# A hybrid transformer block on one core: the 88 products of local attention in 22 sets of four instead of 24 of four and three, with new planner offsets

## The chip, the cores and the metric

The kernel is one program on one core of a Trainium2 chip. The metric is device time in microseconds (us) of one execution. TensorE (PE in the rows; PEld is its weight load), VectorE (DVE), ScalarE (ACT), GpSimd (POOL) and SyncE (SP, which only issues DMAs here) each run their own instruction list and meet at semaphores.

## What is computed

Eight batches of 512 x 256 pass a local attention (stage A), an expert feed-forward (F), a causal attention (B) and the feed-forward again, each with a layer norm before it. The change lies in A:

```python
_OFFSETS = list(range(41)) + [128, 96, 384]      # 44 offsets
idx = arange(T)[:, None] - deltas[None, :]       # T = 512
k_mod = k[:, :, max(idx, 0)] * (1.0 + scale_embed)
scores = einsum('bhtd,bhtjd->bhtj', q, k_mod) / sqrt(HD) + pos_bias    # H = 16, HD = 16
scores = where(idx >= 0, scores, finfo.min)
out = einsum('bhtj,bhtjd->bhtd', softmax(scores), v[:, :, max(idx, 0)]) * if_gain
```

## The kernel before

Stage A is called once per batch (eight calls), B eight times, F sixteen times. In A, channels stand on partitions, in two halves (hf) of 8 heads. For each of the 44 offsets (slots) and each half, VectorE multiplies qT by kT shifted by the offset, 512 columns: 88 products per call (L1302 to L1308). Four of them (or three) are one set: one VectorE instruction makes all near slots of a set (their offsets are equally spaced, so one access pattern reads them), and each far slot (41 to 43) needs its own. TensorE then sums each product over the 16 channels of a head with the narrow weights slot_w, 32 columns wide, into one quarter of a bank's partitions (L1623 to L1627): the products of a set use different column tiles of the array and run together. Each matmul is two instructions (fp32). A bank holds a group of up to 16 slots: 4 column tiles by 4 rounds, 8 heads each, so 128 partitions. The third group has 12 slots, laid out as 3 column tiles by 4 rounds, on 96 partitions (GROUP_J, L22; PRODUCTS, L66; SETS, L70). The last set of a group is followed by a matmul of is_slot and ahead, which puts -1e30 where t is less than the offset (L1632); ScalarE then copies the bank to sT with the position bias (L1086). There are 24 sets in a call, 16 of four and 8 of three.

Then for each of four tiles of 128 rows, "tS": TensorE turns the three groups of each half (L1600), VectorE takes the maximum per head over 44 slots (L1262) and subtracts it (L1265), ScalarE takes the exponential ("p"), SyncE writes the near slots to a band in DRAM (L897) and reads it back skewed (L909), GpSimd adds the far slots, and TensorE multiplies the turned weights with V.

Product buffers: sets 0 to 5 alternate between two, later sets between four (SET_AT, L75), and a product waits until TensorE has used the set that was there (L1301).

The order of every engine's instructions is made ahead by a planner in the file (ordered(), L498): each phase has an estimated time per engine (local_phases(), L149), and a list scheduler picks the next block by its earliest start, rounded to TICK, and then by its rank times DEPTH plus fixed pulls per phase (PULL) and per call (CALL_PULL). Calls of A, B and F interleave by this: while one batch's attention makes products, another's experts use TensorE. The planner also gives each result one of eight PSUM banks. The setup makes slot_w from a mask and the scales (L1483).

Of the kernel before, what the change touches and what calls it, by code (L numbers as in the profile page):

```python
# [21 lines left out]
GROUP_J = [16, 16, 12]  # L22
NG = len(GROUP_J)
# [21 lines left out]
def columns(names):  # L45
    at, n = {}, 0
    for name, w in names:
# [18 lines left out]
PRODUCTS = [(hf, g, col, r) for hf in range(2) for g in range(NG) for r in range(4) for col in range(GROUP_J[g] // 4)]  # L66
# [4 lines left out]
        for hf in range(2) for g in range(NG) for r in range(4)]  # L71
# [8 lines left out]
def slot(n):  # L80
    _, g, col, r = PRODUCTS[n]
    return 16 * g + 4 * col + r
# [66 lines left out]
def local_phases():  # L149
# [14 lines left out]
    for q, of in enumerate(SETS):  # L164
# [4 lines left out]
        p.put(("prod", q), ("DVE", 0.067 * len(runs(q)) + 0.534 * len(of), *needs), ("PE", 0.9 if r < 3 else 1.3 if g == NG - 1 else 1.1))  # L169
        if r == 3:  # L170
            p.put(("sT", hf * NG + g), ("ACT", 0.58, ("prod", q, "PE")))
# [4 lines left out]
    for kind, i in TILES:  # L176
        if kind == "tS":
            p.put(("tS", i), ("PE", 0.62, ("v", 1, "PE"), *[("sT", g, "ACT") for g in range(2 * NG)]),
                  ("DVE", 2.0, *([("write", i - 2, "DMA"), ("far", i - 2, "POOL"), ("far_den", i - 2, "DVE")]
                                 if i >= 2 else [])))  # L180
        elif kind == "p":
            p.put(("p", i), ("ACT", 0.68, ("tS", i, "DVE")))
            p.put(("write", i), ("SP", 0.4, ("p", i, "ACT")), ("DMA", 2.6))
            if i > 0:
                for k in (0, 1) if i == 1 else (i,):
                    p.put(("read", k), ("SP", 0.4, ("write", k, "DMA"),
                                        *([("pA", k - 2, 3, "PE")] if k >= 2 else []),
                                        *([("pB", k - 2, 1, "PE")] if k >= 3 else [])), ("DMA", 7.0))
# [142 lines left out]
def calls():  # L331
# [19 lines left out]
TICK, DEPTH = 0.02, 1.55  # L351

PULL = {
    ("A", "DVE"): {"prod": 3430, "on": 470, "pB": 170},
    ("A", "PE"): {"tS": 780, "on": 990, "oNT": 350},
    ("B", "ACT"): {"mT": -1390, "ST": -2340},
    ("B", "DVE"): {"qk": 280, "S": -80, "on": -680},
    ("B", "PE"): {"turn": 1070, "qk": 2960, "S": 4290, "mT": 130, "ST": 1930, "oNT": 1020, "pr": 170},
    ("F", "ACT"): {"gexp": -20},
    ("F", "DVE"): {"stats": 1490, "xn": -150, "cont": -1470, "lg": -300, "gates": -810},  # L360
    ("F", "PE"): {"turn": -620, "hid": 316, "eo": 1710, "dec": 10230},
}
CALL_PULL = {
    "A": [-7420, 0, 0, -510, -460, -300, -60, -157],
    "B": [300, 810, 340, 0, 300, 450, 640, -260],
    "F": [0, 910, -390, 0, -80, 0, -30, 0, 130, 670, 370, 0, 296, 650, 0, 0],
# [249 lines left out]
SLOTS_SETUP, TABLES_SETUP = 5, 11  # L616
DVE_SETUP = 26
# [26 lines left out]
def build(nc, x_dram, kept_dram, setup_dram, out_dram):  # L644
# [9 lines left out]
    with ctx:  # L654
# [179 lines left out]
        def products_used(u, q):  # L834

            if q % 4 == 3:
                return bank_full(u, ("sT", q // 4))
            return nth(u, "prod_used", q - q // 4 + 1)
# [213 lines left out]
        def _(act):  # L1052
# [15 lines left out]
            def local_attention(u, name):  # L1068
# [13 lines left out]
                elif kind == "sT":  # L1082
                    rows = GROUP_J[i % NG] * HPT
                    act.wait_ge(*bank_full(u, name))
                    ps, read = place(u, name)
                    nc.scalar.activation(sT[0:rows, i, :], ps[0:rows, :], ACT.Identity,  # L1086
                                         bias=c("pos_bias", i, 1)[0:rows, :]).then_inc(read, 1)
# [111 lines left out]
        def _(dve):  # L1199
# [51 lines left out]
            def softmax_local(u, i):  # L1251
# [4 lines left out]
                for hf in range(2):  # L1256
                    dve.wait_ge(*bank_full(u, ("tS", i, hf)))
                    ps, read = place(u, ("tS", i, hf))
                    s = ps[:, 0:J * HPT].rearrange("p (j h) -> p j h", j=J)
                    halves.append((s, read))  # L1260
                    m = mx[:, i, hf * HPT:(hf + 1) * HPT]
                    link(u, nc.vector.tensor_reduce(m, s.rearrange("p j h -> p h j"), AX, ALU.max))  # L1262
                for hf, (s, read) in enumerate(halves):
                    m = mx[:, i, hf * HPT:(hf + 1) * HPT]
                    nc.vector.tensor_tensor(p_nat[:, i % 2, :, hf * HPT:(hf + 1) * HPT], s,  # L1265
                                            m.unsqueeze(1).broadcast_to([P, J, HPT]), ALU.subtract
                                            ).then_inc(read, 1)
# [642 lines left out]
```

## Time and profile before

| | us |
|---|---|
| median of 3 runs | 1737.67 |
| lowest, highest | 1734.58, 1738.28 |
| the profiled execution | 1734.03 |
| its span | 1731.9 |
| TensorE busy | 1580.9 (91%) |
| VectorE busy | 1282.0 (74%) |
| ScalarE busy | 787.8 (45%) |
| mean granted TensorE clock | 0.977 of full |

One execution is profiled. A row of the grouped lines names the source line, engine, output and inputs, shape and count, then the busy time together, the mean of one instruction, and the engine's idle time before them with what ended it. Instructions of one engine overlap by their start and end, so the distance between starts is shorter than the duration.

### The profile page before, as it was taken

Reading aid. Unit: us, or ns where it says so; the run is one execution under the profiler, and the core shown is the slowest. Engines: PE = TensorE matmul, PEld = TensorE weight load, DVE = VectorE, ACT = ScalarE, POOL = GpSimd, SP = SyncE. Lnnn points to the kernel's source line nnn. Section 1 sums busy time; section 2 is a strip of 40 time slices with the busy share of each in tenths; the row PEclk is TensorE's granted clock in tenths of the full one; section 3 lists DMA queues with packets and bytes.
Section 4 is the critical chain, followed back from the end, with each engine's and each line's share of the span. In section 5 each row is a group of like instructions: output and inputs, shape, how many; then the busy total and the mean of one; then the engine's idle time right before and its main releaser. Section 6 shows DMA issues by size and latency. Waiting matters only on the chain. (4 is left out here: it accounts for less than half of the span.)

```text
span 1731.9 us, 28223 instructions
## 1 busy us (share of the span) xinstructions
PE 1580.9 (91%) x10560; PEld 882.0 (51%) x10560; DVE 1282.0 (74%) x3138; ACT 787.8 (45%) x1474; POOL 141.6 (8%) x155
## 2 busy tenths in 40 slices
PE   6599899999999999999999999999989998997976
PEld 2164465546555465554654556454655546454533
DVE  7969757896569966798767976699666996746633
ACT  1134346445364544644355353644536444552633
POOL 1010110101101020000101011010200001000000
PEclk9899999999999999999999999999999999998989
DMA  9230440014301161022500244001520216013000
GB/s 318 79 121 1 159 148 2 16 73 172 86 3 39 50 219 40 2 87 86 172 2 15 75 141 117 2 16 74 184 75 3 74 50 207 5 39 111 3 13 13
DMA packets 50261, 133.96 MB, mean 77 GB/s; under 512 B 6256, under 2 KB 22576, under 8 KB 45520
## 3 DMA queue, kind: packets, MB, share of 16 engines
q1 hardware_dynamic: 50128, 132.16, 23.3%
q8 instruction: 87, 1.43, 0.3%
q14 instruction: 46, 0.38, 0.1%
HBM read 80.99 MB, written 46.04 MB: 73 GB/s over the span
## 5 line engine op out<-in xcount | busy, mean ns | idle before, releaser
L1306 DVE TENSOR_TENSOR arena_AB<-qT,kT 128x2048 f32<-128x2048 f32 (+3 forms) x240 | 400.1, 1719 | 11.9 <-PE bank L1625 5.5
L1361 DVE CUSTOM_DVE_ANT_0 bank<-bank,causal_b 128x512 f32<-128x512 f32 (+3 forms) x512 | 234.1, 525 | 105.4 <-PE bank L1697 104.9
L1543 PE MATMUL bank<-arena_F,kept 128*128 128x512 f32 x512 | 235.6, 609 | 7.2 <-DVE arena_F L1451 4.8
L1625 PE MATMUL bank<-arena_AB,slot_w 128*32 128x512 f32 x1408 | 198.1, 612 | 32.6 <-DVE arena_AB L1306 31.4
L1135 ACT ACTIVATE arena_AB<-bank 128x512 f32<-128x512 f32 (+1 forms) x352 | 167.0, 585 | 70.2 <-PE bank L1713 69.8
L1168 ACT ACTIVATE arena_F<-bank,kept 128x512 f32<-128x512 f32 x256 | 159.0, 688 | 20.0 <-PE bank L1543 17.7
L1543 PEld LDWEIGHTS bank<-arena_F,kept 128*128 128x128 f32 x512 | 96.5, 195 | 124.7 <-issue 113.1
L1543 PE MATMUL bank<-cont_hi,by_cont 128*128 128x512 f32 (+1 forms) x272 | 115.9, 426 | 9.6 <-DVE arena_AB L1361 6.5
L1821 PE MATMUL bank<-kept,arena_F 128*128 128x256 f32 x512 | 117.0, 382 | 7.1 <-ACT arena_F L1185 6.6
L1543 PE MATMUL bank<-xnT,kept 128*128 128x512 f32 x256 | 120.0, 622 | 2.2 <-ACT xnT L1060 1.5
L1806 PE MATMUL bank<-arena_F,kept 128*64 128x512 f32 x512 | 120.5, 602 | 0.4 <-ACT arena_F L1181 0.2
L1001 POOL TENSOR_TENSOR rstd_F<-var_eps_F,minus_half 128x4 f32<-128x4 f32 x32 | 40.2, 1256 | 973.8 <-DVE var_eps_F L1236 973.8
L1821 PEld LDWEIGHTS bank<-kept,arena_F 128*128 128x128 f32 x512 | 95.2, 190 | 26.5 <-ACT arena_F L1185 10.4
L1459 DVE TENSOR_TENSOR arena_F<-bank,kept 128x512 f32<-128x512 f32 x32 | 22.1, 691 | 116.8 <-PE bank L1821 116.8
L1543 PE MATMUL bank<-cont_lo,by_cont 128*128 128x512 f32 (+1 forms) x272 | 107.1, 394 | 0.0
L1709 PE MATMUL bank<-arena_AB 99*128 99x256 bf16 (+3 forms) x512 | 103.8, 301 | 0.2
L1625 PEld LDWEIGHTS bank<-arena_AB,slot_w 128*32 128x32 f32 x1408 | 35.2, 109 | 133.6 <-DVE arena_AB L1306 69.6
L1732 PE MATMUL bank<-arena_AB,V_b 128*32 128x512 f32 (+3 forms) x1024 | 87.1, 441 | 10.4 <-ACT arena_AB L1135 8.8
L1697 PE MATMUL bank<-arena_AB 96*128 96x512 bf16 (+3 forms) x512 | 89.3, 310 | 7.4 <-DMA arena_AB<-ones_b 4.1
L1713 PE MATMUL bank<-causal_T,ident_b 128*128 128x128 bf16 (+2 forms) x352 | 86.0, 244 | 0.0
L1543 PEld LDWEIGHTS bank<-xnT,kept 128*128 128x128 f32 x256 | 50.7, 202 | 60.6 <-issue 56.5
L1152 ACT ACTIVATE arena_F<-bank,half_enc_b 128x512 f32<-128x512 f32 x64 | 44.0, 687 | 79.9 <-PE bank L1543 79.9
(186 smaller groups left out, 2359.9 us busy)
## 6 DMA issues: line engine op xcount, KB each, us to landing
arena_AB<-band SPq DMA_DIRECT2D x32, 1344.0 KB, 6.6
arena_AB<-stacks SPq DMA_DIRECT2D x64, 384.0 KB
stacks<-arena_AB SPq DMA_DIRECT2D x48, 256.0 KB, 2.6
band<-arena_AB SPq DMA_DIRECT2D x32, 328.0 KB, 3.9
stacks<-xnT SPq DMA_DIRECT2D x32, 256.0 KB, 2.6
band<-kT SPq DMA_DIRECT2D x4, 1352.0 KB, 23.1
stacks<-xn SPq DMA_DIRECT2D x16, 256.0 KB, 3.0
kept<-kept_pack SPq DMA_DIRECT2D x1, 3765.0 KB, 18.8
```

The costliest lines, as they stand in the source:

```text
L1135: nc.scalar.activation(p_T[:, n % RS, cols[0]:cols[-1] + 1, 0:w], ps[:, 0:len(cols) * w].rearrange("p (c q) -> p c q", c=len(cols)), ACT.E ...
L1168: nc.scalar.activation(hid[:, n % RH, :], ps[:], ACT.Relu, bias=c("be1", n, 1)).then_inc(read, 1)
L1306: ins = nc.vector.tensor_tensor(prod[SET_AT[i]][:, col:col + c, :], qT[:, hf, :].unsqueeze(1).broadcast_to([P, c, T]), k, ALU.mult)
L1361: ins = nc.vector.tensor_tensor_reduce(out=s, in0=s, in1=causal[:, (TT - 1 - i) * P:T], scale=-1.0, scalar=BIG, op0=ALU.add, op1=ALU.min, ...
L1543: ins = nc.tensor.matmul(out(ps), w, x, start=n == 0, stop=n == len(pairs) - 1)
L1625: ins = nc.tensor.matmul(ps[HS * col:HS * (col + 1), :], slot_w[:, slot(n), :], prod[SET_AT[i]][:, col, :], start=r == 0, stop=False, skip ...
L1697: ins = nc.tensor.matmul(ps[:, at:at + (i + 1) * P], stacks[0:K, h // 4, 0, h % 4, i * P:(i + 1) * P], stacks[0:K, h // 4, 1, h % 4, 0:(i ...
L1709: nc.tensor.matmul(ps[:, at * w:(at + 1) * w], stacks[0:K + 3, g, 1, col, k * P:(k + 1) * P], stacks[0:K + 3, g, 0, col, k * P:T], start=a ...
L1713: ins = nc.tensor.matmul(ps[:, 0:number * w].rearrange("p (c q) -> p c q", c=number)[:, :, 0:P], ident_b[:], causal_T[:].unsqueeze(1).broa ...
L1732: ins = nc.tensor.matmul(ps_o[HS * col:HS * (col + 1), k * P:T], V_b[:, k, columns_of(4 * g + col)], p_T[:, n % RS, col, 0:w], start=k == ...
L1806: ins = nc.tensor.matmul(ps[M * e:M * (e + 1), :], we2[:, 2 * n + e, k, :], hid[:, (4 * n + 2 * e + k) % RH, :], start=k == 0, stop=k == 1)
L1821: ins = nc.tensor.matmul(ps[:, i * D:(i + 1) * D], t_moe[:, k, at:at + P], dec_w[:, k, :], start=k == 0, stop=k == KF - 1)
```

## The change

The third group gets four column tiles of three rounds (ROUNDS = [4, 4, 3]). All sets have four products; there are 22 in a call. Slot number, key stride (3 instead of 4 in that group), the last set of a group (LAST) and the semaphore counts follow. The third group's scores now stand on all 128 partitions, 24 of each 32 in use; the unused 8 get a bias of -1e30, so that they are never the maximum. Score transposes, mask matmul and ScalarE's copy lose their 96-row special case. VectorE's maximum reads 384 columns, and its subtraction becomes two instructions, 32 slots and 12 slots, so that p_nat keeps its 44 slots. The planner gets times for band writes and reads per tile, and other TICK, DEPTH, PULL and CALL_PULL.

```diff
 GROUP_J = [16, 16, 12]
+ROUNDS = [4, 4, 3]
...
-PRODUCTS = [(hf, g, col, r) for hf in range(2) for g in range(NG) for r in range(4) for col in range(GROUP_J[g] // 4)]
+PRODUCTS = [(hf, g, col, r) for hf in range(2) for g in range(NG) for r in range(ROUNDS[g]) for col in range(4)]
...
-        for hf in range(2) for g in range(NG) for r in range(4)]
+        for hf in range(2) for g in range(NG) for r in range(ROUNDS[g])]
+LAST = [q for q, of in enumerate(SETS) if PRODUCTS[of[0]][3] == ROUNDS[PRODUCTS[of[0]][1]] - 1]
...
-            p.put(("tS", i), ("PE", 0.62, ("v", 1, "PE"), *[("sT", g, "ACT") for g in range(2 * NG)]),
-                  ("DVE", 2.0, *([("write", i - 2, "DMA"), ("far", i - 2, "POOL"), ("far_den", i - 2, "DVE")]
+            p.put(("tS", i), ("PE", 0.66, ("v", 1, "PE"), *[("sT", g, "ACT") for g in range(2 * NG)]),
+                  ("DVE", 2.2, *([("write", i - 2, "DMA"), ("far", i - 2, "POOL"), ("far_den", i - 2, "DVE")]
...
-            p.put(("write", i), ("SP", 0.4, ("p", i, "ACT")), ("DMA", 2.6))
+            p.put(("write", i), ("SP", 0.4, ("p", i, "ACT")), ("DMA", (2.3, 2.3, 6.3, 5.0)[i]))
...
-                                        *([("pB", k - 2, 1, "PE")] if k >= 3 else [])), ("DMA", 7.0))
+                                        *([("pB", k - 2, 1, "PE")] if k >= 3 else [])), ("DMA", (6.6, 8.3, 6.0, 6.5)[k]))
...
-TICK, DEPTH = 0.02, 1.55
+TICK, DEPTH = 0.04, 2.0
...
-    ("A", "DVE"): {"prod": 3430, "on": 470, "pB": 170},
-    ("A", "PE"): {"tS": 780, "on": 990, "oNT": 350},
-    ("B", "ACT"): {"mT": -1390, "ST": -2340},
-    ("B", "DVE"): {"qk": 280, "S": -80, "on": -680},
-    ("B", "PE"): {"turn": 1070, "qk": 2960, "S": 4290, "mT": 130, "ST": 1930, "oNT": 1020, "pr": 170},
-    ("F", "ACT"): {"gexp": -20},
-    ("F", "DVE"): {"stats": 1490, "xn": -150, "cont": -1470, "lg": -300, "gates": -810},
-    ("F", "PE"): {"turn": -620, "hid": 316, "eo": 1710, "dec": 10230},
+    ("A", "ACT"): {"sT": 300},
+    ("A", "DVE"): {"prod": 2450, "pB": 20},
+    ("A", "PE"): {"tS": 593, "on": 850, "oNT": 720},
+    ("B", "DVE"): {"S": 810, "pr": -160},
+    ("B", "PE"): {"qk": 2210, "S": 2460, "ST": 1840},
+    ("F", "ACT"): {"hid": 10, "gb": 450},
+    ("F", "DVE"): {"stats": 1990, "lg": 80, "eo": -350},
+    ("F", "PE"): {"hid": 473, "dec": 11940},
 }
 CALL_PULL = {
-    "A": [-7420, 0, 0, -510, -460, -300, -60, -157],
-    "B": [300, 810, 340, 0, 300, 450, 640, -260],
-    "F": [0, 910, -390, 0, -80, 0, -30, 0, 130, 670, 370, 0, 296, 650, 0, 0],
+    "A": [-6730, 0, -154, -80, -72, 0, -3, 0],
+    "B": [0, 0, 0, 0, 0, 0, -1180, 0],
+    "F": [0, 0, -77, 0, 0, 0, 4, 0, 0, 0, 74, 0, 100, -360, 520, 0],
...
-                    nc.vector.tensor_tensor(p_nat[:, i % 2, :, hf * HPT:(hf + 1) * HPT], s,
-                                            m.unsqueeze(1).broadcast_to([P, J, HPT]), ALU.subtract
-                                            ).then_inc(read, 1)
+                    p = p_nat[:, i % 2, :, hf * HPT:(hf + 1) * HPT]
+                    nc.vector.tensor_tensor(p[:, 0:whole], ps[:, 0:whole * HPT].rearrange("p (j h) -> p j h", h=HPT),
+                                            m.unsqueeze(1).broadcast_to([P, whole, HPT]), ALU.subtract)
+                    nc.vector.tensor_tensor(
+                        p[:, whole:J].rearrange("p (c r) h -> p c r h", c=4),
+                        ps[:, whole * HPT:NG * P].rearrange("p (c r h) -> p c r h", c=4, r=4)[:, :, 0:ROUNDS[-1]],
+                        m.unsqueeze(1).unsqueeze(1).broadcast_to([P, 4, ROUNDS[-1], HPT]), ALU.subtract).then_inc(read, 1)
...
-                        k = bass.AP(k.tensor, k.offset, [k.ap[0], [4, c], [1, T]])
+                        k = bass.AP(k.tensor, k.offset, [k.ap[0], [ROUNDS[g], c], [1, T]])
...
-                        rows = GROUP_J[g] * HPT
-                        ins = nc.tensor.transpose(ps[:, g * P:g * P + rows], sT[0:rows, hf * NG + g, i * P:(i + 1) * P],
-                                                  ident[0:rows, 0:rows])
+                        ins = nc.tensor.transpose(ps[:, g * P:(g + 1) * P], sT[:, hf * NG + g, i * P:(i + 1) * P], ident)
...
-                        nc.tensor.matmul(ps[0:rows, 0:cut], is_slot[:, g * P:g * P + rows], ahead[:, 0:cut],
+                        nc.tensor.matmul(ps[:, 0:cut], is_slot[:, g * P:(g + 1) * P], ahead[:, 0:cut],
...
+    bias.reshape(4, HS, 2, NG)[:, HPT * ROUNDS[-1]:, :, NG - 1] = NEG
```

The maximum (L1262) changes its input to ps[:, 0:NG * P], and the slot weights of the setup (L1483) are made by two instructions, for 32 slots in rounds of four and for 12 in rounds of three.

## Rows read from the trace of the kernel before

**Rows 1.** the page, its busy times, share of the span, instructions.

```profile
PE 1580.9 (91%) x10560; PEld 882.0 (51%) x10560; DVE 1282.0 (74%) x3138; ACT 787.8 (45%) x1474; POOL 141.6 (8%) x155
```

**Rows 2.** stretches: us, then busy us and (instructions) of PE, PEld, DVE, ACT, POOL, PEclk, DMA.

```profile
43.30:86.60 43.30, 25.25 (x143) 8.49 (x141) 42.18 (x61) 6.28 (x9) 3.77 (x5) 0.85 0.25 79
...
346.40:389.70 43.30, 43.27 (x206) 19.60 (x206) 42.57 (x66) 17.37 (x29) 1.01 (x1) 1.00 0.19 73
389.70:433.00 43.30, 39.84 (x383) 27.86 (x380) 27.97 (x63) 22.72 (x42) 7.17 (x10) 1.00 0.49 172
...
952.60:995.90 43.30, 43.24 (x212) 22.64 (x209) 42.84 (x58) 17.10 (x30) 1.01 (x1) 1.00 0.20 75
...
1645.40:1688.70 43.30, 31.13 (x162) 15.90 (x160) 13.40 (x39) 14.45 (x29) 1.01 (x1) 0.88 0.04 13
...
86.60:1558.80 1472.20, 1394.44 (x9616) 787.29 (x9614) 1122.88 (x2747) 702.91 (x1317) 129.24 (x134) 0.99 0.23 75
```

**Rows 3.** all waits of PE, those of 90 to 1430 us, the product matmuls' busy row.

```profile
PE bank L1625 <- DVE arena_AB L1306: 31.4, 43, 2.7
PE bank L1551 <- DVE xn L1248: 12.5, 2, 9.6
PE bank L1551 <- DVE arena_F L1248: 12.3, 3, 5.6
...
PE bank L1625 <- DVE arena_AB L1306: 13.3, 21, 2.7
...
L1625 PE MATMUL bank<-arena_AB,slot_w 128*32 128x512 f32 x1408 | 198.1, 612 | 32.6 <-DVE arena_AB L1306 31.4
```

**Rows 4.** PE in order of time: start us, us, what, instructions, idle before.

```profile
384.90 1.06 PE L1625 MATMUL bank<-arena_AB,slot_w 128*32 128x512 f32 x6
385.89 0.65 PE L1806 MATMUL bank<-arena_F,kept 128*64 128x512 f32 x2
...
562.76 1.92 PE L1625 MATMUL bank<-arena_AB,slot_w 128*32 128x512 f32 x12
...
573.82 1.92 PE L1625 MATMUL bank<-arena_AB,slot_w 128*32 128x512 f32 x16
```

**Rows 5.** products on DVE: two forms of the grouped lines, one run in time.

```profile
L1306 DVE TENSOR_TENSOR arena_AB<-qT,kT 128x2048 f32<-128x2048 f32 x128 | 287.2, 2287 | 8.9 <-ACT kT L1076 3.4 <-PE bank L1625 3.2 <-PE bank L1713 1.8
...
L1306 DVE TENSOR_TENSOR arena_AB<-qT,kT 128x512 f32<-128x512 f32 x48 | 32.9, 686 | 0.0
...
362.02 15.50 DVE L1306 TENSOR_TENSOR arena_AB<-qT,kT 128x2048 f32<-128x2048 f32 x7
```

**Rows 6.** score transposes by shape, and weight loads of the mask matmul.

```profile
L1600 PE MATMUL bank<-kept,arena_AB 128*128 128x128 f32 x128 | 21.6, 280 | 3.2 <-DVE arena_AB L1265 2.6 <-ACT arena_AB L1086 0.7
...
L1600 PE MATMUL bank<-kept,arena_AB 96*128 96x96 f32 x64 | 16.1, 251 | 0.0
...
L1632 PEld LDWEIGHTS bank<-ahead,is_slot x48: 94/96/120, 31.1 to 1417.3; 128*128 128x128 bf16 x32, 128*96 128x96 bf16 x16
```

**Rows 7.** score subtraction, a 256-column subtraction's like, two subtractions in time.

```profile
L1265 DVE TENSOR_TENSOR arena_AB<-bank,arena_AB 128x352 f32<-128x352 f32 x64 | 30.6, 520 | 1.1
...
L1277 DVE TENSOR_TENSOR oN<-bank,arena_AB 128x256 f32<-128x256 f32 x32 | 13.6, 424 | 1.1
...
407.03 0.96 DVE L1265 TENSOR_TENSOR arena_AB<-bank,arena_AB 128x352 f32<-128x352 f32 x2
```

**Rows 8.** the first local call: VectorE in time, then one set on PE.

```profile
18.36 4.50 DVE L1306 TENSOR_TENSOR arena_AB<-qT,kT 128x2048 f32<-128x2048 f32 x2 [3.43 <-ACT kT L1076]
25.55 44.69 DVE L1306 TENSOR_TENSOR arena_AB<-qT,kT 128x2048 f32<-128x2048 f32 x28 [2.70 <-PE bank L1625]
...
38.91 1.07 PE L1625 MATMUL bank<-arena_AB,slot_w 128*32 128x512 f32 x8 [1.14 <-DVE arena_AB L1306]
```

**Rows 9.** us to landing of band writes (L897), then of band reads (L909).

```profile
DMA to landing us min/median/max: 2.2/3.9/8.4
...
DMA to landing us min/median/max: 5.5/6.6/9.2
```

## Prediction: what 22 sets of four do to the time

> **What bounds the kernel now.** I read the page's busy lines first [rows 1]: TensorE is busy 1580.9 of 1731.9 us, VectorE 1282.0. 151 us of TensorE idleness are left. Then the table by stretches [rows 2] says where: between 87 and 1559 us TensorE is busy 1394 of 1472 us, so 78 us of idleness lie there and 73 at the two ends. In the first product stretch (43 to 87 us) VectorE is busy 42.18 of 43.30 us and TensorE only 25.25: there VectorE bounds. In later product stretches (346 to 390, 953 to 996 us) both are full: TensorE 43.27 and 43.24, VectorE 42.57 and 42.84. In the score and band stretch behind (390 to 433 us) VectorE has 15 us of slack. Last, the waits of TensorE [rows 3]: product matmuls waited 31.4 us for VectorE's products in the whole run, but 13.3 us in 21 waits between 90 and 1430 us, where seven of the eight local calls have theirs. So outside the first call TensorE's work and VectorE's work both count, TensorE's a little more, and work moves between stretches only by the planner's order.
>
> **Part 1, two product sets fewer per call.** A set of three column tiles (6 matmul instructions) alone takes 1.06 us, one of four (8 instructions) 1.07 [rows 4, 8]. Two sets of three in a row take 1.92 us, two of four 1.92 [rows 4]. So a set costs 1.92 - 1.06 = 0.86 us in a row, and alone 0.99 (from its start at 384.90 to the next work's at 385.89), whatever its number of columns. Before, a call has 24 sets, 8 of them of three; after, 22 of four. TensorE loses 2 sets: 1.72 to 1.98 us per call; I take 1.85, as sets stand in both ways.
> The Trainium skill ("TensorEngine Tiling (Array Packing)", Key Properties) says that a change of tiling mode drains TensorE. By that each set that stood alone would give back a drain besides; the difference 0.99 - 0.86 = 0.13 us is all that the trace shows of one, and 1.85 lies inside it.
>
> **Part 2, VectorE's products.** The products stay 88. A full set in a row costs 2.20 us: seven end 15.50 us after the first starts, one takes 2.287, so (15.50 - 2.29) / 6 [rows 5]. 2048 elements against 512 differ by 2287 - 686 ns, or 1.04 ns per element, hence 2.13 us of elements and 0.07 fixed. In the third group a half had 7 instructions (3 columns; three times 2 and 1), and gets 6 (three times 3 and 1, since slots 41 to 43 are single). Saving 2 x 0.07 = 0.13 us per call.
>
> **Part 3, scores.** The third group's rows fill 128 partitions, the unused ones with a bias of -1e30, so score tiles get 384 columns. On TensorE a transpose of 96 rows takes 251 ns, one of 128 rows 280 [rows 6]: 8 per call by 0.029 = +0.23 us, and not under zero, since the weight load has 128 columns in both. The closing mask matmul gets 128 instead of 96 weight columns, its 384 moving columns stay; weight loads of both widths lie between 94 and 120 ns [rows 6]: nothing, at most 2 x 0.03. ScalarE's copy with bias gets 128 partitions for 96 and keeps its 512 columns: nothing.
> On VectorE the maximum reads 384 instead of 352 columns: 32 x 1.04 = 33 ns. The subtraction becomes two instructions of 256 and 96 columns; two of 352 in a row end 0.96 us after the first starts and one takes 0.52, so a step of 0.44 us holds 0.37 of elements and 0.07 fixed [rows 7]. The split adds 0.07 us. Upper bound: no overlap at all, a whole 256-column instruction 424 ns plus 96 columns scaled from there, 257 ns, against 520: +0.16. With 8 pairs per call: 8 x (0.033 + 0.07) = +0.82 us, at most 1.5. VectorE's net is 0.82 - 0.13 = +0.7 us per call, and almost all of it in the score stretch, not among the products.
> The Trainium skill ("VectorE: DVE Perf Modes", Side-by-side) speaks against the split: it gives each instruction some 150 cycles of start at 0.96 GHz, which would be an estimated 64 x 0.16 = 10 us for the 64 extra subtractions. The step above disagrees: all but 0.07 us lies under the instruction before [rows 7], so 64 x 0.07 = 4.5 us. By the page a quarter of the other 5.5 us, 1.4 us, would come on top of the sum below.
>
> **Part 4, setup and bookkeeping.** The slot weights come from two instructions instead of one, +0.1 us by the fixed part above. VectorE idles 3.43 us before the first product, waiting for the keys [rows 8]: hidden. Semaphore indices change, no new wait arises; product buffers are reused two and then four sets back as before.
>
> **Part 5, the planner.** The band writes get 2.3, 2.3, 6.3, 5.0 us instead of 2.6, the reads 6.6, 8.3, 6.0, 6.5 instead of 7.0; the trace has 2.2 to 8.4 (median 3.9) and 5.5 to 9.2 (median 6.6) [rows 9], so the planner's picture is nearer to the chip. But all pulls, the tick and the depth change too, so every engine's order changes, that of the other two stages as well; on SyncE and GpSimd each band write, read or far sum can come to stand behind another call's wait. No row prices a new order. From above: the waits of TensorE that a better order could take are 5 to 13 us per kind [rows 3]; I take -10 as the gain's end. From below: one badly placed normalisation costs up to 9.6 us (xn) or 5.6 us (the experts'), as the longest waits before the transposes show [rows 3]. I take 0, since no row speaks for either side.
>
> **Sum against the profiled execution** (span 1731.9, whole 1734.03 us). First call: VectorE bounds it, its products follow each other for 44.69 us while TensorE waits before each set [rows 8]; two sets less on TensorE give nothing, and of VectorE's +0.7 I take +0.5, as its score steps have TensorE's transposes to wait for, too. The seven others: TensorE -1.85 + 0.23 = -1.6 each, -11.3 together. 21 of their 168 sets waited for VectorE, and in the fullest stretches VectorE has under 1 us left, so I count 0.8 of it: -9.0. VectorE's +0.8 per call lies where it has slack, but on the chain score transposes, maximum, subtraction, exponent, band write, band read; I charge a quarter: +1.4. Sum -7.1, so 1726.9 for the profiled execution. It ran 3.6 us under the median of the three runs; against that median the sum gives 1737.67 - 7.1 = 1730.6. Rounded **1730.5 us**, -0.41%.
>
> **Rivals.**
> (a) *The sum holds, order neutral*: 1724 to 1734, around 1730.5. For it: the exactly equal times of the set of three and of four. Chance 0.48.
> (b) *The new order gains besides.* With the later band landings the planner no longer puts head transposes where TensorE waits for the band, and the other calls close up: -7 and another -8 to -10, 1720 to 1722. For it: the 78 us of idleness in the middle [rows 2]. Against it: no single wait kind there is over 13.3 us. Chance 0.16.
> (c) *VectorE is the true bound of the product stretches, TensorE's freed time becomes waits for products.* For it: the VectorE column in [rows 2]. Then the rows "matmul of products waited for VectorE" grow by some 10 us and the time stays: 1737.67 + 7 x 0.2 = about 1737 to 1739. Chance 0.16, within 0.2% of before.
> (d) *Slower: the new order breaks hand-overs at the normalisation.* The place: the VectorE queue, where the normalisation of the next call stands behind products or score maxima, and TensorE's first transposes wait for it. The price is 5.6 us each (the experts' longest [rows 3]) with the clock at its lower level behind: in the stretch from 1645 us, where TensorE has gaps, the mean granted clock is 0.88 of 2.4 GHz, part of it at 1.2, against 1.00 in the full ones [rows 2]. It decides from two such new gaps on: -7.1 + 11.2 = +4, 1742 us; with three 1747. For it: all offsets change at once and the calls' pulls are mostly zero now. Against: the sixteen expert calls of before show such gaps only at the ends. Chance 0.20.
> That the change does not do what it says (fewer TensorE sets) is next to impossible by the code; that it does so without shortening anything is (c).
>
> **How the numbers follow.** A difference of 0.2% (3.5 us) is about what a measurement of this kernel can tell from no change. (a) is nearly all faster, one part in twenty within 0.2%; (b) faster; (c) within; (d) slower but for a small part. Faster 0.63, same 0.18, slower 0.19. Range: from (b)'s lower half, 1719.5, to 1741.5, which takes in (c) and the near side of (d); left out are about 0.05 below and 0.12 above, with the case of three gaps.
>
> **What would show it right or wrong.** The product matmuls stay 1408 instructions, in 22 sets of 8 per call, and are busy for 198.1 - 14 = about 184 us. VectorE makes the products with 16 instructions fewer, all sets with 1536 or 2048 columns in the first. The product sets' times on VectorE fall by about 2 us in all. The subtraction shows 64 of 256 and 64 of 96 columns with a step of 0.07 us between. TensorE's busy time falls by 11 to 13 us to about 1569. If the span falls by less than that, TensorE's idle time has grown: in waits for products it is (c), in waits for normalised tiles (d). The granted clock of full stretches should stay 1.00. The prediction is wrong if the time moves while TensorE's busy time does not fall, or if the score transposes come over 20 us later behind the products.

## The result

The changed kernel takes 1743.0 us (median of 12 runs, 1741.2 to 1745.5) against 1737.7 for the kernel before, measured anew beside it: a ratio of 1.0034, 95% interval 1.0026 to 1.0042. Forecast were 1730.5 us and a range up to 1741.5. The kernel became slower, by 5.9 us by the ratio and 5.3 by the medians, where a gain of 7 was forecast.

The page of the changed kernel, its busy times (answers to [rows 1]):

```profile
span 1741.7 us, 28222 instructions
PE 1574.4 (90%) x10544; PEld 877.6 (50%) x10560; DVE 1288.8 (74%) x3187; ACT 791.2 (45%) x1474; POOL 143.9 (8%) x155
```

TensorE is busy 6.5 us less, the span is 9.8 us longer, so it idles 167 instead of 151 us. (The profiled execution of before lies 3.6 us under its median, that of the changed kernel 0.7 over it, so some 4 of the 9.8 us are the choice of executions.) The stretches of the changed kernel (columns as in [rows 2]):

```profile
43.30:86.60 43.30, 24.13 (x146) 7.63 (x143) 42.23 (x63) 6.19 (x9) 3.71 (x5) 0.84 0.17 54
...
346.40:389.70 43.30, 42.74 (x207) 20.52 (x206) 42.74 (x58) 19.15 (x34) 1.01 (x1) 1.00 0.20 73
389.70:433.00 43.30, 40.65 (x360) 26.93 (x357) 32.03 (x78) 22.53 (x41) 6.43 (x8) 1.00 0.46 168
...
952.60:995.90 43.30, 42.58 (x213) 21.51 (x212) 42.72 (x60) 16.16 (x29) 1.01 (x1) 1.00 0.22 82
...
86.60:1558.80 1472.20, 1382.12 (x9571) 780.97 (x9587) 1127.95 (x2785) 703.09 (x1312) 131.63 (x134) 0.99 0.23 75
```

Between 87 and 1559 us TensorE is busy 12.3 us less than before and idle 12.3 us more: nothing of what it was relieved of became progress there. In the two full product stretches VectorE is as full as it was (42.74 and 42.72 us for 42.57 and 42.84), TensorE a little less (42.74 and 42.58 for 43.27 and 43.24).

The groups of the changed kernel that answer to [rows 3, 6] (line, engine, what, count, then busy, mean ns, idle before):

```profile
L1636 PE MATMUL bank<-arena_AB,slot_w 128*32 128x512 f32 x1408 | 183.9, 613 | 37.4 <-DVE arena_AB L1316 36.0
...
L1612 PE MATMUL bank<-kept,arena_AB 128*128 128x128 f32 x192 | 24.1, 275 | 2.7 <-DVE arena_AB L1274 2.0 <-ACT arena_AB L1093 0.7
```

One half's subtraction in time (start us, us), which answers to [rows 7]:

```profile
402.55 0.42 DVE L1272 TENSOR_TENSOR arena_AB<-bank,arena_AB 128x256 f32<-128x256 f32 x1
402.89 0.25 DVE L1274 TENSOR_TENSOR arena_AB<-bank,arena_AB 128x96 f32<-128x96 f32 x1
```

The instructions cost what the forecast said: the sets 183.9 us for 184 expected, 14.2 less; the second part of the subtraction starts 0.34 us after the first, 0.27 of which are its 256 columns, so 0.07 is fixed. TensorE's busy time fell to 1574.4 us, though, and not to 1569. Two groups that the change does not touch grew, with unchanged counts and a longer mean. They are the matmuls of the experts' and of both attentions' normalised input; the changed kernel, then what they were before:

```profile
L1556 PE MATMUL bank<-arena_F,kept 128*128 128x512 f32 x512 | 239.8, 617 | 10.0 <-DVE arena_F L1461 5.0
...
L1556 PE MATMUL bank<-xnT,kept 128*128 128x512 f32 x256 | 124.0, 635 | 3.6 <-ACT xnT L1068 2.3
```

```profile
L1543 PE MATMUL bank<-arena_F,kept 128*128 128x512 f32 x512 | 235.6, 609 | 7.2 <-DVE arena_F L1451 4.8
...
L1543 PE MATMUL bank<-xnT,kept 128*128 128x512 f32 x256 | 120.0, 622 | 2.2 <-ACT xnT L1060 1.5
```

One execution each does not carry much here. In runs below that keep the order of before, the second group takes 120.0 to 123.8 us, and the new layout in the order of before has TensorE busy for 1573.0 us in one run and 1568.6 in another of the same time. The first group takes 235.6 to 236.8 us in the old order and 237.7 to 239.8 in four runs with the new numbers or their order, so 1 to 4 us of it may belong to them. Nor does the granted clock of single stretches tell the kernels apart: the changed kernel, the kernel before, and the kernel before with nothing but its subtraction split, whose order is that of before (a few us later in its work by then):

```profile
1472.20:1515.50 43.30, 41.18 (x179) 21.23 (x181) 30.71 (x115) 22.14 (x40) 0.00 (x0) 0.92 0.09 23
...
1472.20:1515.50 43.30, 42.26 (x198) 21.10 (x197) 31.08 (x117) 24.20 (x44) 0.00 (x0) 0.99 0.02 4
...
1472.20:1515.50 43.30, 41.39 (x190) 21.38 (x191) 33.11 (x131) 22.21 (x40) 1.02 (x1) 0.92 0.17 45
```

Over all runs the mean granted clock is 0.973 for the changed kernel (12 runs) and 0.976 for the kernel before (the 19 runs beside the first experiments). So a little more of TensorE's work met the lower level (1.2 GHz); how much of the 5 us that is stays open.

### The profile page after: what moved, and what is told of

Read it like the earlier page. It is cut to its first block and busy times, and to the rows that moved or that the text cites. A ratio compares the mean times of both kernels' runs of the same rounds, so it can differ in the third digit from the quotient of the medians.

```text
span 1741.7 us, 28222 instructions
## 1 busy us (share of the span) xinstructions
PE 1574.4 (90%) x10544; PEld 877.6 (50%) x10560; DVE 1288.8 (74%) x3187; ACT 791.2 (45%) x1474; POOL 143.9 (8%) x155
## 3 DMA queue, kind: packets, MB, share of 16 engines
q1 hardware_dynamic: 50128, 132.16, 23.1%
## 5 line engine op out<-in xcount | busy, mean ns | idle before, releaser
L1316 DVE TENSOR_TENSOR arena_AB<-qT,kT 128x2048 f32<-128x2048 f32 (+1 forms) x224 | 397.6, 1829 | 10.7 <-PE bank L1636 5.3
L1556 PE MATMUL bank<-arena_F,kept 128*128 128x512 f32 x512 | 239.8, 617 | 10.0 <-DVE arena_F L1461 5.0
L1636 PE MATMUL bank<-arena_AB,slot_w 128*32 128x512 f32 x1408 | 183.9, 613 | 37.4 <-DVE arena_AB L1316 36.0
L1556 PE MATMUL bank<-xnT,kept 128*128 128x512 f32 x256 | 124.0, 635 | 3.6 <-ACT xnT L1068 2.3
L1009 POOL TENSOR_TENSOR rstd_F<-var_eps_F,minus_half 128x4 f32<-128x4 f32 x32 | 44.1, 1379 | 1003.2 <-DVE var_eps_F L1242 1003.2
```

The lines of the kernel that those rows point to most:

```text
L1316: ins = nc.vector.tensor_tensor(prod[SET_AT[i]][:, col:col + c, :], qT[:, hf, :].unsqueeze(1).broadcast_to([P, c, T]), k, ALU.mult)
L1556: ins = nc.tensor.matmul(out(ps), w, x, start=n == 0, stop=n == len(pairs) - 1)
L1636: ins = nc.tensor.matmul(ps[HS * col:HS * (col + 1), :], slot_w[:, slot(n), :], prod[SET_AT[i]][:, col, :], start=r == 0, stop=False, skip ...
```

## The experiments

Two theories stood after the result. **Order**: the layout gains what the sum said and the new offsets cost more. **Layout**: the freed TensorE time can't be used and VectorE's added work decides.

### Layout and order apart

The first run takes the order of every engine and every bank from the planner of before, with its 24 sets, and drops one place of the third group; the second does the reverse. (Edits here and below are shortened; notes behind # are not in the files.)

```diff
+def moved(q):                                    # e5: places of the old plan to new sets
+    hf, k = divmod(q, 12)
+    ... {8: [8], 9: [], 10: [9], 11: [10]} ... else 11 + ...
+def moved(q):                                    # e6: places of the new plan to old sets
+    hf, k = divmod(q, 11)
+    return [12 * hf + x for x in {8: [8, 9], 9: [10], 10: [11]}.get(k, [k])]
```

> The new layout (22 sets of four, split subtraction, 384-column scores) in the instruction order of the kernel before: every engine's list and every bank is taken from the planner of before with its 24 sets, and the second of the four sets of the third group is left out of both lists, so that the other three keep their places. Theory 'order' (the layout gains what the sum said, the new offsets cost more): 1729 to 1732 us, ratio about 0.996, TensorE busy near 1569. Theory 'layout' (VectorE's 0.7 us per call and the larger products decide, the freed TensorE time is not usable): 1740 to 1744 us, ratio 1.002 to 1.004. In between, 1735 to 1739: the freed time is lost in waits, and only a part of the loss is the layout's.

> The other half: the old layout (24 sets, 16 of four and 8 of three) in the instruction order and with the banks of the changed kernel; the fourth set of the third group is put right behind the first of that group. Theory 'order': 1747 to 1752 us, since the layout's 7 us are missing as well. Theory 'layout': 1735 to 1739 us, as before.

Measured: the layout in the old order 1742.3 us (1.0029, 1.0016 to 1.0043); the old layout in the new order 1750.4 us (1.0082, 1.0065 to 1.0099). The first is what the layout theory expected, the second what the order theory expected, so neither holds alone. In the order of before the layout **costs 4.7 us** (5.0 by the ratio); in the order of the change it **gains 7.4** (1750.4 to 1743.0). Each layout does relatively better in the order that was planned for it, so these are prices in an order that fits one side only.

Then the planner plans each layout with the other's numbers:

```diff
-TICK, DEPTH = 0.04, 2.0         # e1: the changed kernel with all planner numbers of before
+TICK, DEPTH = 0.02, 1.55        # (PULL, CALL_PULL, write 2.6 and read 7.0 likewise)
...
-TICK, DEPTH = 0.02, 1.55        # e2: the kernel before with all planner numbers of the change
+TICK, DEPTH = 0.04, 2.0
```

> The new layout planned anew by the planner with the numbers of before: old tick, depth and pulls, old band landings. Theory 'order': the offsets were made for 24 sets, so the plan is another one, but 1730 to 1738 us, below the changed kernel. Theory 'layout': 1740 to 1745 us. A time above 1745 would say that the offsets only fit one plan, whatever the layout.

> The old layout planned anew with the tick, depth, pulls and band landings of the change. Theory 'order' (these numbers are worse in themselves): 1745 to 1752 us. Theory 'layout': 1736 to 1740 us. If it comes near 1743 as the changed kernel does, layout and numbers can't be told apart by replanning alone, and the pair that keeps an order decides.

Measured: 1733.9 us for the new layout with the old numbers (0.9984, 0.9974 to 0.9995) and 1763.1 us for the old layout with the new ones (1.0148, 1.0128 to 1.0168). With numbers that were not chosen for it, the new layout gains 3.8 us over the kernel before (2.8 by the ratio). **The changed kernel's own numbers cost it 9.1 us against the old ones** (1733.9 to 1743.0; the kernel before stood at 1737.6 and 1737.7 beside them). They are bad for the old layout too, by 25 us, more than either theory had expected (1745 to 1752 or less). Planning the new layout for itself, with the same old numbers, takes it from 1742.3 to 1733.9 us: the 4.7 us above are the price in an order that was made for the other layout. And the 3.8 us are those of one plan; plans of this layout range from 1727.5 to 1760.2 us below.

### What a microsecond is worth in the old order

Why does the layout cost 4.7 us in the old order? The page of that run, its waits for products (us, times, longest), and those of 90 to 1430 us:

```profile
PE 1573.0 (90%) x10544; PEld 879.8 (51%) x10560; DVE 1288.1 (74%) x3187; ACT 787.8 (45%) x1474; POOL 141.4 (8%) x155
```

```profile
PE bank L1678 <- DVE arena_AB L1358: 43.5, 59, 2.7
```

```profile
PE bank L1678 <- DVE arena_AB L1358: 26.1, 39, 2.7
```

TensorE waits 12 us more for products than in [rows 3], all of it in the middle, where the waits went from 13.3 us in 21 to 26.1 in 39. Four runs take the change apart. The first has the layout with VectorE's score work of before, the second the kernel before with the split subtraction, the others the kernel before with less work on one engine each:

```diff
-                    whole = 16 * (NG - 1)        # e7, on top of e5: one subtraction of 352
+                    nc.vector.tensor_tensor(p_nat[...], ps[:, 0:J * HPT]..., m..., ALU.subtract)
...
-                    nc.vector.tensor_tensor(p_nat[...], s, m..., ALU.subtract)      # e8
+                    for at, to in ((0, 32), (32, J)):
+                        ins = nc.vector.tensor_tensor(p_nat[:, i % 2, at:to, ...], s[:, at:to], m..., ALU.subtract)
...
-                    for n in SETS[i]:                                               # e10
-                        col = PRODUCTS[n][2]
+                    short = g == NG - 1 and r == 1
+                    for n in SETS[i][0:1] if short else SETS[i]:
+                        col, w_ = PRODUCTS[n][2], 64 if short else T
...
+                        w_ = T // 2 if g == NG - 1 and r == 1 else T                # e11
```

> The new layout in the order of before, but VectorE's score work as before: maximum over 352 columns and one subtraction of 352 (the 12 slots of the third group are then read from the wrong columns; the work is what counts). It takes 0.8 us per call off VectorE. Theory 'score chain' (the 4.7 us that the layout cost in this order are VectorE's added score work): 1735 to 1738 us. Theory 'products' (the cost is that the third group's products come in three larger portions and TensorE waits for them): 1740 to 1742 us, nearly as with the full layout.

> The kernel before with one edit: the subtraction in two instructions, 32 and 12 slots, 64 instructions more. Theory 'score chain': +3 to +5 us, 1741 to 1743. Theory 'products': 0 to +1 us. The step of the second subtraction behind the first should be 0.07 us beyond its elements; by the page that gives each instruction 150 cycles it would be 0.16 us.

> The kernel before with the summing of the second set of the third group left out but for one matmul of 64 columns: TensorE has 16 times some 0.7 us less, about 11 us, VectorE, order, waits and banks are untouched. If a microsecond of TensorE counts in the product stretch: 1729 to 1732 us. If VectorE's products set the pace there, as TensorE's 43.5 us of waits for products in the run with the layout alone suggest: 1735 to 1738 us, and the waits for products grow by 8 us or more.

> The counterpart: VectorE multiplies only 256 of 512 columns in the second set of the third group, 16 times 0.8 us, about 13 us less, and everything on TensorE is as before (the sums of the other half are then of an older product). If VectorE sets the pace of the product stretches: 1726 to 1731 us. If TensorE does: 1734 to 1738 us.

| run | VectorE busy | TensorE busy | ratio to before (95%) | us |
|---|---|---|---|---|
| layout, old score work | 1283.7 | 1575.7 | 1.0006 (0.9994 to 1.0017) | +1.0 |
| before, split subtraction | 1285.7 | 1581.0 | 1.0019 (1.0009 to 1.0029) | +3.3 |
| before, less on TensorE | 1281.6 | 1572.1 | 0.9974 (0.9962 to 0.9986) | -4.5 |
| before, less on VectorE | 1270.2 | 1579.6 | 0.9987 (0.9978 to 0.9997) | -2.3 |

Here and below us is the ratio's difference from 1 times 1737.5. The score chain is confirmed from both sides: taking VectorE's score work away returns 4.0 of the layout's loss, and the split alone, 3.7 us of VectorE, costs 3.3. That is some nine tenths (0.4 to 1.4 by the interval); the forecast charged a quarter. By which wait it costs that is not shown: TensorE's waits for products are 32.7 us with the split for 31.4 without, and those of the middle 26.0 us without the layout's score work for 26.1 with it. The run with less on TensorE falls between its two expectations: 8.8 us less busy gain 4.5, so half (0.3 to 0.75), where the forecast counted 0.8. Its waits (all, then 90 to 1430 us) show where the other half went:

```profile
PE bank L1626 <- DVE arena_AB L1306: 38.2, 52, 2.7
```

```profile
PE bank L1626 <- DVE arena_AB L1306: 20.0, 31, 2.7
```

6.8 us more waits for products than in [rows 3]. And 11.8 us less on VectorE gain only 2.3, a fifth (0.04 to 0.3), with TensorE's waits for products where they were, 31.6 us. So neither engine alone bounds the product stretch.

There remains a gap: with its score work taken away the layout should gain like the run with less on TensorE, 4.5 us or more, and stands at +1.0 (interval -1.0 to +3.0). The portions are different: the third group's four sets of three (VectorE 1.8 to 1.9 us each) became three of four (1753 + 685 ns, 2.4 us). Three runs look at that:

```diff
-    ... {8: [8], 9: [], 10: [9], 11: [10]} ...    # e15, on top of e5: another place left out
+    ... {8: [], 9: [8], 10: [9], 11: [10]} ...
...
+                    if (g, r) == (NG - 1, 1): ... 8 columns instead of the set's products and sums   # e16
...
+                        more = g == NG - 1 and r != 1 and run == runs(i)[-1]                          # e17
+                        c += int(more)
```

> As the run with the layout alone (1742.3 us), but of the third group's four places in the lists the first is left out, not the second: its three sets of four stand at the second, third and fourth. VectorE then has the time of four places for three larger portions. Theory 'portions' (TensorE comes to the larger portions before they are made): the waits for products fall from 43.5 towards 36 us, the time to 1738 to 1740. Theory 'place does not matter' (VectorE's sum of work counts): 1741 to 1744 us with the waits as they were.

> The kernel before with the second set of the third group left out on both engines (8 columns stay of it, so that waits and increments stand): VectorE 16 times some 1.6 us less, about 25 us, TensorE 16 times 0.8 us less, about 12. If the prices of the two runs with less work on one engine add and scale (TensorE 0.5 us of time per us of its work, VectorE 0.2): -11 us, 1726 us. If one engine hides the other's part, so that only both together free the path: -15 us or more, 1722 or less.

> The kernel before with a fourth product made, and used by nobody, in the other three sets of the third group: VectorE 48 times 0.53 us more, 25.6 us, TensorE nothing. This run and the one above together are what the new layout does to the products in the old order. Theory 'VectorE's microseconds are worth the same everywhere in the group' (0.2): +5 us, 1743. Theory 'portions' (work in the portions that TensorE comes for is worth more): +10 to +15 us, 1748 to 1753; with -11 above that leaves what the layout without its score work showed, +1.

Measured: another place left out, 1742.5 us (1.0028, 1.0018 to 1.0038), waits for products 46.1 us: which place is left out does not matter, and this form of the portions theory falls. A set left out on both engines: 0.9939 (0.9926 to 0.9952), -10.6 us, near the 11.5 to which the two single prices add up (13.3 us less on TensorE, 24.5 on VectorE). A fourth product in three sets, TensorE untouched: 1.0123 (1.0110 to 1.0136), **+21.4 us for 25.5 us of VectorE**. Two stretches of this run:

```profile
346.40:389.70 43.30, 40.25 (x199) 20.35 (x203) 42.78 (x59) 14.34 (x25) 1.01 (x1) 1.00 0.24 87
952.60:995.90 43.30, 40.45 (x254) 21.96 (x251) 41.76 (x72) 19.09 (x37) 3.98 (x2) 1.00 0.24 84
```

VectorE is as full as in [rows 2], TensorE has lost 3 us in each. In the whole trace TensorE idles 168 us for 151 and is, for the same work, busy 1590.5 us for 1580.9, with a mean granted clock of 0.973 over the runs for 0.976; so a part of the price is longer matmuls and not waits. The time is above both expectations (1743, and 1748 to 1753). Work added to three of the sets costs 0.84 us per microsecond (0.75 to 0.93), work taken from the fourth gains 0.2. The two differ in the place and in the direction, and no run separates these; in the score work the price was 0.9 in both directions. The last two runs together give +10.8 us, the layout without its score work +1.0: they do not add, and why is not shown. TensorE's waits for products between 90 and 1430 us say where the gap lies, in the layout without its score work and in the run with the fourth product:

```profile
PE bank L1674 <- DVE arena_AB L1354: 26.0, 39, 2.7
...
PE bank L1627 <- DVE arena_AB L1308: 26.9, 40, 2.7
```

The run that only takes work off TensorE has 20.0 us there, the layout without its score work 6.0 us more, which is about the size of the gap (5.5 us). So the larger portions show as waits for products, and the score work hardly does.

### What is wrong with the new numbers

The last expert calls' final additions (start us, us, engine), changed kernel:

```profile
1540.16 1.67 DVE L1483 SCALAR_TENSOR_TENSOR x_second<-arena_F,rstd_F,x_second 128x256 f32<-128x256 f32 x4
...
1646.45 1.67 DVE L1483 SCALAR_TENSOR_TENSOR x_first<-arena_F,rstd_F,x_first 128x256 f32<-128x256 f32 x4
...
1736.55 1.67 DVE L1483 SCALAR_TENSOR_TENSOR x_second<-arena_F,rstd_F,x_second 128x256 f32<-128x256 f32 x4
```

and the kernel before:

```profile
1534.52 1.67 DVE L1473 SCALAR_TENSOR_TENSOR x_second<-arena_F,rstd_F,x_second 128x256 f32<-128x256 f32 x4
...
1646.49 1.67 DVE L1473 SCALAR_TENSOR_TENSOR x_first<-arena_F,rstd_F,x_first 128x256 f32<-128x256 f32 x4
...
1726.77 1.67 DVE L1473 SCALAR_TENSOR_TENSOR x_second<-arena_F,rstd_F,x_second 128x256 f32<-128x256 f32 x4
```

The changed kernel is 5.6 us behind after the third last expert call, level after the second last, 9.8 behind at the end. In its list 62 blocks of the last causal call stand on TensorE behind the decoding of the second last expert call, 44 in the kernel before; the last expert call hangs on them. Does the tail lose the 10 us?

```diff
-    "B": [0, 0, 0, 0, 0, 0, -1180, 0],
+    "B": [0, 0, 0, 0, 0, 0, 0, 0],
```

> The changed kernel with one number of the planner changed: the pull of the seventh causal call, -1180, is 0. In TensorE's list 47 instead of 62 blocks of the last causal call then stand behind the decoding of the last expert call but one (44 in the kernel before). Theory 'tail' (the changed kernel's last 10 us are lost because the last causal call, on which the last expert call hangs, stands behind): the distance of the two last expert calls' ends falls from 90 to 82 us and the time to 1735 to 1739. Theory 'trade' (what the tail gets back, the calls before it lose): the distance falls, the time stays at 1742 to 1745.

Measured: 1745.4 us (1.0049, 1.0035 to 1.0062). The distance of the last two fell from 90.1 to 87.8 us, less than expected, and the time did not fall: the third last expert call now ended at 1546.4 instead of 1541.8. It is a trade, not a loss; the theory of the tail falls. (The changed numbers buy an early second last call with a late last one; what they lack is the progress before.)

The band landings by themselves, with the old tick, depth and pulls:

```diff
-            p.put(("write", i), ..., ("DMA", 2.6))             # on top of e1
+            p.put(("write", i), ..., ("DMA", (2.3, 2.3, 6.3, 5.0)[i]))
```

> The new layout with the old tick, depth and pulls (1733.9 us with the old band landings), but with the landings of the band as the change gives them. Theory 'landings help' (they are nearer to the trace, so the plan fits better): 1729 to 1733 us. Theory 'numbers are fitted together' (any one of them changed gives another plan to which the others were not fitted): 1738 us or more, perhaps 1750.

Measured: 1760.2 us (1.0142, 1.0122 to 1.0163), **26 us more** than the same kernel with the landings that are further from the trace. Its waits of TensorE show a kind that no run above has in this size:

```profile
PE bank L1564 <- DVE arena_F L1254: 17.4, 4, 5.6
PE bank L1564 <- DVE arena_AB L1371: 14.7, 6, 9.2
```

The longest of these waits, TensorE and then VectorE in time:

```profile
1285.87 1.94 PE L1564 MATMUL bank<-kept,arena_F 128*128 128x128 f32 x8 [9.15 <-DVE arena_AB L1371]
...
1279.30 1.41 DVE L1235 BATCH_NORM_STATS2 stats_AB<-x_second 128x6 f32<-128x256 f32 x4 [3.24 <-DMA x_second<-x]
...
1281.23 1.37 DVE L1254 TENSOR_SCALAR arena_F<-x_first,mv_F,rstd_F 128x256 f32<-128x256 f32 x4
```

The transposes of a normalised tile need that tile and a free bank. In VectorE's list their tile stands behind the statistics of another batch, whose load had not landed (3.24 us idle), and the wait ends when a score maximum of the causal stage has read a bank. A likely reading is that the pulls were fitted to one plan and another landing time makes another plan to which they do not fit.

The planner could have been asked. ordered() in each kernel file works out an end time for every block by the planner's estimates; the largest of them is when the plan ends:

| kernel | its plan ends at, us | measured, us |
|---|---|---|
| before | 1722.9 | 1737.7 |
| changed | 1723.8 | 1743.0 |
| new layout, old numbers | 1719.5 | 1733.9 |
| old layout, new numbers | 1736.9 | 1763.1 |
| new layout, old pulls, new landings | 1740.7 | 1760.2 |
| changed, one pull at 0 | 1727.0 | 1745.4 |

For the change as a whole the plan ends 0.9 us later, where the forecast said 7 us earlier; for the new layout with the old numbers it ends 3.4 us earlier (measured 3.8), with the new landings 21.2 us later than that (measured 26.3). So of the 9.1 us that the new numbers cost the new layout, 4.3 are in the plan itself (1719.5 to 1723.8); what makes the other 4.8 on the chip is not shown. The four plans with the new landings are measured 18 to 26 us above their own end, the two with the old ones 14 to 15 (and the two searched plans below, also with the old ones, 16 and 20): the estimates nearer to the trace did not bring the plan nearer to the chip.

Last, two plans searched from the old numbers with the same effort, half an hour of random steps in the pulls, judged by the planner's own measure: one for the new layout, one for the old.

```diff
-    "A": [-7420, 0, 0, -510, -460, -300, -60, -157],          # e14, the main ones
-    "F": [0, 910, -390, 0, -80, 0, -30, 0, 130, 670, 370, 0, 296, 650, 0, 0],
+    ("A", "DVE"): {..., "far_den": 463, "stats": -4395},
+    ("B", "PE"): {"turn": 4085, ..., "mT": -884, "PV": -1490},
+    "A": [-7420, 0, 0, -510, -460, -300, -60, -1166],
+    "F": [0, 910, -390, 0, -80, -998, -1903, 0, 130, 670, 370, 0, -1119, 650, -7, 0],
...
+    ("A", "DVE"): {"prod": 3409, ..., "stats": -4403},        # e18, the main ones
+    ("F", "DVE"): {..., "gates": -2673},
+    "F": [-2002, 910, -390, 245, -80, 620, -30, 0, 130, 670, 370, 587, 296, 650, 0, 0],
```

> The new layout, old landings, with pulls searched from the old ones by the planner's own measure of its plan, about half an hour. If the planner's measure is good to some us, as the other plans suggest, it beats 1733.9: 1725 to 1731 us. If the rest between plan and chip is larger than the gain of the search: 1731 to 1738.

> The old layout with pulls searched from its own for the same half hour, by the same measure, as the searched plan of the new layout (1727.5 us). Theory 'search' (the gain of that plan is the search's, not the layout's): 1726 to 1730 us as well. Theory 'layout' (with a plan made for it the new layout is worth its TensorE time): 1732 to 1737 us.

Measured: the new layout **1727.5 us (0.9937, 0.9925 to 0.9950), 10.9 us faster than before and 15.5 faster than the change**; the old layout 1740.3 us (1.0015, 1.0005 to 1.0024), slower than its old plan. The planner's own ends are 1711.4 and 1719.9 us: by its measure the search found 8.1 us on the new layout and 3.0 on the old, and the chip gave back 6.4 and none. The second time lies above both its expectations. The page of the first:

```profile
span 1723.3 us, 28240 instructions
PE 1566.9 (91%) x10544; PEld 882.0 (51%) x10560; DVE 1284.9 (75%) x3187; ACT 789.2 (46%) x1474; POOL 143.6 (8%) x155
```

TensorE's busy time is within 2 us of the 1569 that the forecast had, and its idle time, 156 us, is near the old 151. So the layout's gain can come through in a plan that lets it. How much of the 10.9 us is the layout's and how much luck of one search can't be told from one search each.

## Why the prediction was wrong, point by point

- **What bounds the kernel.** Right that both engines count in the product stretches, wrong by how much. "TensorE's a little more" was 0.5 us of time per microsecond of TensorE against 0.2 of VectorE when work is taken from one set, and 0.84 for VectorE when work is added to the three others.
- **Part 1**, the sets: right, 14.2 us less in 16 sets, 0.89 each.
- **Part 2**, the products: 400.1 to 397.6 us on VectorE, 2.5 less, where the sum had 8 x 0.13 = 1.0 and the list of signs about 2. It left out that the same work now comes in fewer, larger portions; that was no term of the sum, and some 5 us in the old order may hang on it.
- **Part 3**, the score work: its size right (0.07 us per split; the Trainium skill's 150 cycles in "VectorE: DVE Perf Modes", Side-by-side, would have made it 0.16, which the trace does not bear out). Its price wrong: it was charged a quarter, because VectorE has slack in that stretch, and cost nine tenths (3.3 us for 3.7). A stretch's mean slack did not give the price of the chain maximum, subtraction, exponential, band; which wait in it decides is open. On TensorE the transposes grew by 1.0 us (23.1 to 24.1) for 1.9 in the sum.
- **Part 4**, setup: not tested by itself; VectorE still waits for the keys before the first product (4.4 us, [rows 8] 3.43).
- **Part 5**, the planner: the step that failed most. It was set to 0, with landings nearer to the trace named as a point in favour. The numbers cost 9.1 us on this layout, 25 on the old one, and the landings alone, among the old pulls, 26. Rows did not price the order, but the planner's own plan did: it ends 0.9 us later than before. Which step failed most hangs on the path: by way of the new layout planned with the old numbers, the numbers cost 9.1 us and the sum for the layout was off by 3.3 (-7.1 for -3.8); by way of the new layout in the old order, the new order costs 0.7 and the sum was off by 11.8. The first path is the one on which both plans are made for their layout.
- **The sum.** TensorE's 0.8 should have been about 0.5 (-5.7 instead of -9.0), the score work's quarter about nine tenths (+5 instead of +1.4), the portions some +5, all in the old order; that gives about the +4.7 measured there, but the last term is the rest that was missing, so the agreement confirms nothing by itself. Planned anew, with the old numbers, the layout stands at -3.8.
- **The rivals.** The time came out as (d) had it, 1742, but not by its mechanism: the waits for normalised tiles grew only from 24.8 to 27.4 us. The number was luck. A wait of that kind, though behind a load and a bank, is in the run with the new landings. What the changed kernel shows is nearest to (c), product waits of 36.0 us for 31.4 and 12 us more idle time in the middle, in a plan that on top makes less progress in the middle than the old numbers give. (b) did not come: the one plan that gains beyond the sum of the layout is the searched one, with the old landings, at 1727.5 us and not 1720 to 1722.

## What to carry over

In a kernel whose order was fitted, do not take one price per engine: a microsecond of VectorE was worth 0.2 in one place and direction, 0.84 in others and 0.9 in the score work, and only runs with work added or left out told so. A layout should be judged under an order made for it and one kept from before; a change that moves layout and fitted numbers together hides a good part behind a bad one. A planner's time made truer by itself can cost more than it corrects; that the pulls beside it had taken up its error is the likely reason, not a shown one. And where a planner makes the order, read off when its plan ends before calling the order neutral.

## What was not expected of the hardware

Two VectorE instructions in a row overlap all but 0.07 us: 248 ns for 96 columns, of which the step after it shows 0.16 to 0.17. Transposes of 128 rows instead of 96 cost little: all 192 were busy for 24.1 us instead of 23.1, with a mean of 275 ns for 270 (280 and 251 in the two forms). The mask matmul with 384 columns took 336 ns with 128 weight columns and 363 with 96, so the wider one is no slower. And the granted clock of one and the same stretch, 1472 to 1516 us, was 0.99 in the kernel before and 0.92 in that kernel with nothing but the split added, a few us later in the same order, so a stretch's clock from one trace each says little of a change.
